# Both halves of the attention scores in four PSUM banks, one behind the other

## What is computed

```python
lat = layer_norm(layernorm(x));  ctx = layer_norm(context)
q = (lat @ Wq) -> 16 heads of 64;  k, v = split(ctx @ Wkv) -> 16 heads of 64
k = apply_rope(k, cos, sin)                       # x1*cos - x2*sin, x2*cos + x1*sin
attn = softmax(clip(q k^T * 64**-0.5, -11, 11))   # per head, over 512 context rows
x = x + ((attn @ v) @ Wo + bo)
# second layer
q2 = h@Wq + bq;  k2, v2 = (h@Wdown + bdown)@Wup + bup      # h = rmsnorm(layernorm(x))
att2 = softmax(q2 k2^T / sqrt(8)) over 16 heads of the same token
x1 = ln(x) + (att2 v2)@Wo + bo
x = x + x1 + sum_e gate_e * (h2 @ We_e)                    # gate = softmax(h2@Wg + bg)
```

## Time and profile before

| | us |
|---|---|
| median of 3 runs (309.35 to 309.47) | 309.43 |
| the profiled execution, its own time | 309.32 |
| its span from the first to the last instruction | 307.5 |
| TensorE busy | 291.8 (95%) |
| VectorE busy | 247.5 (80%) |
| GpSimd busy | 208.3 (68%) |
| TensorE weight loads | 203.8 (66%) |
| ScalarE busy | 162.8 (53%) |
| mean granted clock of TensorE | 0.998 |

### The profile page before, as it was taken

How to read it: one execution, slowest core, us unless ns; L and a number is a source line. 1 busy time by engine, 2 the same in 40 slices (tenths; PEclk the granted TensorE clock), 3 DMA queues, 4 the chain that set the end, 5 groups by cost and what they waited for, 6 DMA issues and landing times.

```text
span 307.5 us, 6728 instructions
## 1 busy us (share of the span) xinstructions
PE 291.8 (95%) x2534; PEld 203.8 (66%) x2534; DVE 247.5 (80%) x448; ACT 162.8 (53%) x324; POOL 208.3 (68%) x209
## 2 busy tenths in 40 slices
PE   6889999999999999999999999999999999999983
PEld 6776666766678767666787676566787665576651
DVE  3877999977775869899878788976856699887875
ACT  3637554668543735664516456774436368414532
POOL 7446864666464839876756677599927588878763
PEclk9999999999999999999999999999999999999999
DMA  7554412211110111111111111011201200000001
GB/s 241 163 149 106 124 32 71 56 46 38 43 45 17 37 34 36 37 34 36 43 28 34 37 27 43 16 41 27 51 9 35 53 3 0 2 17 0 3 0 34
DMA packets 15568, 14.24 MB, mean 46 GB/s; under 512 B 3825, under 2 KB 11057, under 8 KB 15537
## 3 DMA queue, kind: packets, MB, share of 16 engines
q1 hardware_dynamic: 15008, 13.49, 16.8%
q10 hardware_dynamic: 528, 0.33, 0.4%
HBM read 4.89 MB, written 0.52 MB: 18 GB/s over the span
## 4 chain that ended last, share of the span: by engine, by line
PE 61%; DVE 14%; POOL 9%; ACT 6%; issue 6%; SPq 2%; DMA 1%; POOLq 0%; DVEq 0%; ACTq 0%
PE pv L662 13%; PE sc L646 12%; PE sums L683 6%; PE pj_k L584 5%; PE side L774 4%; PE pj_k L586 3%; PE pj_k L585 3%; POOL moe L1955 3%; PE side L850 2%; POOL e L1881 2%; SPq L551 2%; ACT e L971 2%; PE side L761 2%; POOL prod L1291 2%; DVE ksin L1399 2%
## 5 line engine op out<-in xcount | busy, mean ns | idle before, releaser
L1881 POOL TENSOR_SCALAR e<-e 128x1024 f32<-128x1024 f32 x64 | 71.8, 1123 | 54.2 <-ACT e L971 46.4
L971 ACT ACTIVATE e<-sc 128x1024 f32<-128x1024 f32 x64 | 65.6, 1025 | 32.1 <-PE sc L646 31.7
L646 PEld LDWEIGHTS sc<-qs,ks 64*128 64x128 f32 x768 | 49.6, 185 | 21.6 <-issue 18.0
L646 PE MATMUL sc<-qs,ks 64*128 64x256 f32 x768 | 62.5, 295 | 0.3 <-ACT e L971 0.3
L662 PE MATMUL pv<-e,v 128*64 128x256 f32 x496 | 60.4, 385 | 0.5 <-POOL e L1881 0.4
L1874 POOL TENSOR_TENSOR krot<-kcos,kswap 128x512 f32<-128x512 f32 x32 | 43.6, 1364 | 13.9 <-DMA kswap<-ksin 9.6
L662 PEld LDWEIGHTS pv<-e,v 128*64 128x64 f32 x496 | 32.9, 136 | 21.4 <-issue 4.5
L979 ACT ACTIVATE u<-pv 128x256 f32<-128x256 f32 x31 | 11.9, 385 | 53.9 <-PE pv L662 47.9
L1335 DVE TENSOR_TENSOR ks<-krot,ks 128x512 fp32r<-128x512 f32 x32 | 32.2, 1005 | 0.0
L963 ACT ACTIVATE v<-pj_k 128x512 f32<-128x512 f32 x28 | 16.8, 598 | 15.1 <-PE pj_k L586 14.7
L1399 DVE TENSOR_TENSOR ksin<-pj_k,sinT 128x512 f32<-128x512 f32 x32 | 21.9, 684 | 3.5 <-PE pj_k L586 2.9
(11 more groups left out here) (303 smaller groups left out, 573.0 us busy)
## 6 DMA issues: line engine op xcount, KB each, us to landing
kswap<-ksin SPq DMA_DIRECT2D x126, 64.0 KB, 2.0
ctx_in<-in_ctx_dram SPq DMA_DIRECT2D x4, 256.0 KB, 3.5
prod<-in_L_xattn_Wkv_dram SPq DMA_DIRECT2D x2, 512.0 KB, 5.1
prod<-in_L_xattn_Wq_dram SPq DMA_DIRECT2D x1, 512.0 KB, 4.7
wo<-in_L_xattn_Wo_dram SPq DMA_DIRECT2D x1, 512.0 KB, 4.5
fwe<-in_L_ffn_We_dram SPq DMA_DIRECT2D x1, 512.0 KB, 4.3
x_in<-in_x_dram SPq DMA_DIRECT2D x1, 384.0 KB, 5.3
out_dram<-x_in SPq DMA_DIRECT2D x3, 128.0 KB, 1.9
```

The costliest lines, as they stand in the source:

```text
L646: last = nc.tensor.matmul(sc[:, h, c * NT:(c + 1) * NT], ks[rows, j % 3, k_part, chunk], qs[rows, j % 2, q_part, :], start=(k_part + q_par ...
L971: nc.scalar.activation(e[:, j % 3, :, 2 * half:2 * half + 2, :].rearrange("p h c n -> p h (c n)"), sc[:, :, :], ACT.Exp, scale=SCALE).then ...
L1881: nc.gpsimd.tensor_scalar(a, a, EXP_HIGH, EXP_LOW, ALU.min, ALU.max).then_inc(s_clip, 1)
```

## The change

The scores get four banks, and all other products of a slot share these or use the banks left:

- `sc` becomes two tensors of two banks, `sc[0]` for the first half and `sc[1]` for the second. `pj_k` is no longer memory of its own but the two banks of `sc[1]`.
- Both halves of the scores of a slot stand behind each other on TensorE, and both exponentials on ScalarE.
- Outputs (`outputs_bank`) go to the first bank of `sc[0]`, queries (`query_bank`) to its second, each after the slot's first exponential has read it; values to the first bank of `sc[1]` after the second exponential. Keys have the bank `pv` to themselves; the first three keys, the first two queries and the first four value units use banks that are free at the start.
- Outputs, queries and values are read by ScalarE alone: `query_hi` makes a second, unrounded copy `q_whole` in SBUF, and `query_lo` on VectorE subtracts from that.
- TensorE's slot reads: `scores(slot, 0)`, `scores(slot, 1)`, side step "d", `sums(slot-1)`, `times_values(slot-1)`, side step "a", `queries(slot+2)`, `values`, side step "b", `keys(slot+3)`, side step "c". Queries are made two slots ahead, one value unit stands in every slot.
- `times_values(slot-1)` waits for the first exponential of the slot, the first half of the next scores for the copies of outputs and of queries, the second half for the copy of the values.
- ScalarE: `key_hi(slot+1)` behind both exponentials (before: `key_hi(slot+2)` at the end of the slot). VectorE: `key_products(slot+2)` (before `slot+3`), `add_chunks` of both halves at the end of the slot. GpSimd: `rotate(slot+2)` behind both clips (before: ahead of them).
- The start and the last two slots are written out anew; norm0 moves from place "a" to "d", lat_T one slot earlier.

```diff
-PREP_STEPS = {(3, "b"): "ctx_T", (6, "a"): "lat_T"}
+PREP_STEPS = {(3, "b"): "ctx_T", (5, "b"): "lat_T"}
...
-        sc = es.enter_context(nc.psum_tensor("sc", [128, 2, 512], fp32))
-        sc_bank = [sc[:, h, :] for h in range(2)]
+        sc = [es.enter_context(nc.psum_tensor(f"sc{half}", [128, 2, 512], fp32)) for half in range(2)]
+        sc_bank = [sc[0][:, h, :] for h in range(2)]
+
+        pj_k = [sc[1][:, h, :] for h in range(2)]
...
-            return sc_bank[0] if j == NPAIR - 1 else pv_bank
+            return pv_bank if NPAIR - 4 < j < NPAIR - 1 else sc_bank[0]
...
+            return (pj_k[0], sc_bank[0], sum_bank)[j] if j < KEYS_AHEAD else pv_bank
...
+            return (pj_k[1], own_bank)[j] if j < QUERIES_AHEAD else sc_bank[1]
...
+                    pe.wait_ge(s_kmul, 2 * j)
...
+                    pe.wait_ge(s_exp, 2 * (j - QUERIES_AHEAD) + 1)
...
+                if n >= SC or n == 2:
+                    pe.wait_ge(s_exp, 2 * slot + 2)
...
-                if j or half:
-                    pe.wait_ge(s_exp, 2 * j + half)
+                    if j:
+                        pe.wait_ge(s_exp, 2 * j - 1)
...
+                    if 2 <= j < NPAIR - 1:
+                        pe.wait_ge(s_u, j - 1)
+                    if 1 <= j < NPAIR - 1:
+                        pe.wait_ge(s_qhi, j + QUERIES_AHEAD)
+                else:
+                    if j:
+                        pe.wait_ge(s_exp, 2 * j)
...
-                elif j:
+                elif j == NPAIR - 2:
                     pe.wait_ge(s_u, j)
...
+                    pe.wait_ge(s_exp, 2 * j + 3)
...
+            for slot in range(NPAIR - 2):
+                scores(slot, 0)
+                scores(slot, 1)
+                side_at(slot, "d")
...
+                if PAIRS < slot and slot % 2 == 0:
+                    sums(slot - 1)
+                times_values(slot - 1)
+                if slot <= PAIRS and slot % 2 == 0:
+                    sums(slot - 1)
+                side_at(slot, "a")
+                if slot + QUERIES_AHEAD < NPAIR:
+                    queries(slot + QUERIES_AHEAD)
+                for n in value_units(slot):
+                    values(n, slot)
+                side_at(slot, "b")
                 if slot + KEYS_AHEAD < NPAIR:
...
             j = NPAIR - 2
             scores(j, 0)
-            queries(j + 1)
+            scores(j, 1)
             sums(j - 1)
-            scores(j, 1)
+            scores(j + 1, 0)
+            scores(j + 1, 1)
             side_at(j, "a")
-            scores(j + 1, 0)
+            times_values(j - 1)
+            sums(j + 1)
             side_at(j + 1, "a")
...
-                nc.scalar.activation(qs[:, j % 2, 0, :], query_bank(j)[:, 0:NT], ACT.Copy).then_inc(s_qhi, 1)
+                    act.wait_ge(s_qlo, j - 1)
+                nc.scalar.activation(qs[:, j % 2, 0, :], query_bank(j)[:, 0:NT], ACT.Copy)
+                nc.scalar.activation(q_whole[:, j % 2, :], query_bank(j)[:, 0:NT], ACT.Copy).then_inc(s_qhi, 1)
...
+                exps(slot, 0)
+                exps(slot, 1)
+                side_taken(slot, "d")
...
+                    key_hi(slot + 1)
                     attention_copy(slot - 1)
...
-                split_lo(qs[:, j % 2, 1, :], query_bank(j)[:, 0:NT], qs[:, j % 2, 0, :]).then_inc(s_qlo, 1)
+                split_lo(qs[:, j % 2, 1, :], q_whole[:, j % 2, :], qs[:, j % 2, 0, :]).then_inc(s_qlo, 1)
...
-                if 0 <= slot + KV_AHEAD < NPAIR:
-                    rotate(slot + KV_AHEAD)
                 second_layer(slot, -1)
...
+                if slot + KV_AHEAD < NPAIR:
+                    rotate(slot + KV_AHEAD)
```

More of the change, by code:

```diff
@@ L161, in side_step @@
     return None
+PLACES = ("d", "a", "b", "c")
 FIRST_BANKS = {("cos_T", 0): 3, ("sin_T", 0): 2, ("lat_T", 0): 3}
@@ L172, in side_order @@
     steps = list(FIRST_STEPS)
-    for slot in range(-KEYS_AHEAD, AFTER + 1):
-        for at, pos in ((slot - 1, "c"), (slot, "a"), (slot, "b")):
-            if side_step(at, pos) and at < AFTER:
-                steps.append(side_step(at, pos))
+    for slot in range(AFTER):
+        for pos in PLACES:
+            if side_step(slot, pos):
+                steps.append(side_step(slot, pos))
     banks = {(name, b): k for name, b, k in TAIL_STEPS}
@@ L921, in _ @@
-            times_values(j)
             times_values(j + 1)
@@ L1781, in _ @@
                                                 AX, ALU.add))
-                if not after_outputs(slot):
-                    side_taken(slot, "a")
-                second_layer(slot, "early")
-                if 1 <= slot + 1 < NPAIR:
+                if slot and slot + 2 < NPAIR:
+                    key_products(slot + 2)
+                side_taken(slot - 1, "c")
+                if slot + 1 < NPAIR:
                     query_lo(slot + 1)
@@ L1788, in _ @@
                     split_latT(b + 1)
-                if after_outputs(slot):
-                    side_taken(slot, "a")
-                if 1 <= slot + 1 < NPAIR:
+                if more and p == 4:
+                    split_ctxT(b + 1)
+                second_layer(slot, "first")
+                side_taken(slot, "d")
+                second_layer(slot, "early")
+                side_taken(slot, "a")
+                if slot + 1 < NPAIR:
                     key_lo(slot + 1)
@@ L1809, in _ @@
                 second_layer(slot, "end")
-                if 0 <= slot < PAIRS:
-                    add_chunks(slot, 0)
+                if slot < PAIRS:
+                    for half in range(2):
+                        add_chunks(slot, half)
             side_taken(AFTER - 1, "c")
```

207 lines of the change are left out of this document (73 added, 134 removed), and 2 rows, old and new, of the table POST_STEPS.

## The result

The changed kernel takes 322.7 us (median of 4 runs, 321.6 to 324.6) against 309.45 (309.35 to 309.62) for the one before on the same chip: a ratio of 1.043, 95% interval 1.038 to 1.048. It is 13.3 us slower, where 308.1 was forecast and the range ended at 314.5. The profiled execution took 324.57 us, 15.3 more than the one before.

A forecast was written before the change was run, and what follows sets the result against it. TensorE was taken as the bound, a full queue over 29 slots. Stages -0.1, slot 0 -0.5, tail -1.4 and lock +0.7 summed to -1.3, applied to the median 309.43: 308.1 us; range 303 to 314.5.

The forecast's parts named there:

- 0.9, 1.4 and 1.6 for ScalarE's lateness: Exponentials held up on ScalarE: 0.9 us lost after slot 6, 1.4 in slot 15, 1.6 in slots 22 to 24.
- I take 0.7, near the low end: VectorE's key step held up by GpSimd through the shared port lock: 0.7 us, between bounds 0 and 8.0.
- the key step has about 1 us to spare: Reason given for the low lock price: in the chained slots VectorE's key step has about 1 us of slack.
- inputs are needed 2 us later: Slots 1 to 8: less TensorE idleness for inputs; 1.1 us kept for two transposes, stage 52.9 before ScalarE's lateness.
- lat_T one slot earlier: nothing: Moving lat_T one slot earlier was priced at nothing, because its source is a slot old.
- -1.4: The tail, from the scores of slot 30 to the first norm product: 15.9 us instead of 17.3.
- Its transfer has then landed: GpSimd's rotation, moved behind both clips, finds its transfer landed, and PV no longer queues behind it.
- B: Slower rival: VectorE becomes the bound, its key step can't run ahead; 8.0 for 0.7 gives 315.4, half 311.8; chance 0.27.
- The sign that was named for B: Scores that wait for VectorE's key step, or keys that wait for its products, would show the slower rival.
- A: Rival: ScalarE is never late before PV, VectorE catches up, the 0.9 + 1.4 + 1.6 vanish: 304.2; chance 0.19.
- C: Rival within 0.2%: the pair of score halves costs 1.80 in ten slots, +1.6: 309.7; chance 0.11.
- D: Rival: PV finds the exponential done, 19 holes fewer, 10 us off: 298; chance 0.03.

## Why the prediction was wrong

**What held.** Two halves behind each other cost 1.62 (1.64 said). The product with the values starts 2.19 after the slot's start with a hole of 0.50 (2.19 and 0.55); there are 18 such waits (19), most of 0.5, in slots 7, 14, 15 and 23 of 1.1 to 1.6. Slots without sums or late engines take 6.0 to 6.2, with sums 7.31 (6.01, 7.32). Slot 0 took 6.35 (6.2). TensorE's prices, block by block, were right. That the stages come out at 53.6, 62.8 and 68.0 with the causes below undone, where the sum had 53.8, 62.7 and 67.9, is in part luck: the sum holds 0.9, 1.4 and 1.6 for ScalarE's lateness, which that run mostly takes away, and without them it had 52.9, 61.3 and 66.3.

**The lock.** "I take 0.7, near the low end" is the term that was mis-sized, and the step that failed first. The 0.7 was the price of the key step alone; the query step got none, and was said to stay near 416 ns, though by the rule of the Trainium skill that stands beside the term it would be held up too. It took 787, which costs VectorE 11.9 us, and the key step's 142 ns more cost it another 4.5. In the kernel before the query step from SBUF costs 4.8 of time. The argument "the key step has about 1 us to spare" looked at one step in chained slots; the longer steps reached TensorE there by the projection bank and by late key products, mostly in slots 3 and 15. In the changed kernel, where the bank doesn't wait for the step, taking the query step off VectorE gave 2.9.

**The term that was missing.** The prediction laid the list out as scores, sums, values, side step "a", and priced it for TensorE only. It said of the new order that inputs are needed 2 us later, and never asked who reads the outputs of a step that moved: side step "a" stood about 1.0 into the slot (slots 10 and 12) and now stands behind the values, 4.1 to 5.4 into it. VectorE works in order, stands 25.6 us in front of it (4.3 before; 27.9 against 18.4 with the side steps that follow), and its key step, for which the next scores wait, is queued behind that. This costs 4.6 alone in the kernel before, and 3.2 to 4.5 come back when it is undone. How VectorE's lateness reaches TensorE is only in part by the key step (6.2 us of waits, 3.5 of them at the end). The rest comes by ScalarE's late exponentials, by the split of `latT` (2.4) and by side products.

"lat_T one slot earlier: nothing" left out that the queries, made two slots ahead, need that split sooner. And some 2.0 of the 4.6 in the kernel before are TensorE's own blocks in the other order, which the prices of the prediction don't hold.

**ScalarE.** The 1.4 and 1.6 for late exponentials in slots 15 and 22 to 24 were put down as losses of their own. The waits are there, but moving those exponentials gained nothing: VectorE set these slots.

**The end.** "-1.4" became +4.7. "Its transfer has then landed" failed in slot 29, where the rotation came 6.7 us after the key products, but VectorE was no earlier itself: its list kept it until 1.0 after TensorE had run dry, and then the key step took 2.33 where 0.68 is the least. With side step "a" early the rotation came 4.7 after the products, and the scores of slot 31 waited 2.8 all the same. From the first scores of slot 30 to the norms it took 22.15, 6.3 more than the 15.9 said: the wait of 3.5, and 2.8 in three blocks at the lower clock (1.2 for the scores, 0.9 for the experts, 0.6 for the values). This is the slowest execution, and a part of the loss at the clock may be its own.

**The rivals.** B had the sign and the engine: VectorE became the bound, scores waited for its key step, hold-ups reached them. Its price of 8.0 was all lock, though; of the 13.3 some 4.5 are side step "a", which is in no rival. (Half of that price in place of 0.7 makes 311.4, not 311.8.) The sign that was named for B, keys waiting for their products, isn't in the trace. B's reason, that the key step can't run ahead any more, is not shown: at the end VectorE itself was late, and the runs that moved the keys ahead again were all slower, though none moved the keys alone. A's gain could not come, since VectorE didn't catch up; C and D are refuted by 1.62 and the 18 waits.

**What stays open.** Undoing single parts gives 2.9, 0.1 and 4.5, in sum 7.5, all together 9.5: where one engine is no longer late another part shows, and the 13.3 can't be shared out exactly. How much the wait of the values for the exponential costs by itself was not measured, as the attempts to fill the hole all moved something dearer. Nor was the second copy of the queries timed without the step that reads it. The rest of 3 us is seen to lie behind the first scores of slot 30; why GpSimd's clips are that late there was only read from the trace, not tried.

## What to carry to other kernels

When an order on one engine is rewritten, list for every step that moved the engines that read its result, and what stands behind that read in their queues; on an in-order engine a step that comes 4 us later can become as much idleness in front of it. An operand moved from PSUM to SBUF is not free for an engine that another one can hold up: price it by the mean of the steps in the trace that already read SBUF only, not by the PSUM one. And an engine at 80% of the span may have no slack at all in the stages that matter.

## What the runs showed of the hardware

- A VectorE subtraction of 128x256 takes 416 ns on average with one operand in PSUM, hardly varying, with both in SBUF 405 at least, 787 on average and 2231 at most. In both kernels with this step no VectorE step from SBUF that overlaps no instruction of GpSimd took over 425 ns (128x256) or 684 (128x512); every longer one overlaps one.
- 16 matmuls into two groups of 32 output rows take as long (1.85 us) as 32 into four (1.86).
- After TensorE had stood for 3.54 us the granted clock was 0.69 over the next 10 us, a mean of its levels of 2.4 and 1.2 GHz; after 4.34 us it was 0.68 over 5.4 us. In the run with the query step from SBUF, waits of 1.69 us in slot 3 and of 0.75 and 1.18 in slot 15 were followed by 0.78 and 0.77 over 7.5 us, with projection matmuls of 0.63 us each, where 0.40 is usual. Blocks in these stretches took up to 1.8 times as long (2.86 for 1.62, 3.05 for 1.88), so a long wait is paid more than once.
